# Eleven stage barriers of a four-layer graph network without GpSimd's drain

## The reference, cut to what matters

```python
edge_index = jnp.stack([src, dst])                       # 25,000 edges over 50,000 nodes
x = _layernorm(x + L0(x, W, gamma, beta, edge_weight, src, dst))      # weighted sum, matmul, norm, relu
x = _layernorm(x + L1(x, edge_index, edge_type_16, W1, root1, ...))   # two relational layers, mean per relation
x = _layernorm(x + L2(x, relation_emb, fc_w, fc_b, edge_index, edge_type_24, 2))  # two attention hops
x = _layernorm(x + L3(x, src, dst, edge_weight, W1, b1, W2, b2))      # interaction, leaky relu, unit length
```

## The kernel before, in words

| stage | what | Block | POOL's indirect DMAs |
|---|---|---|---|
| const | constants | L321 | none |
| sort | edges into buckets, records scattered | L475 | 380 scatters |
| weights | combined weights | L2272 | none |
| l0 | layer 0 | L815 | 410 gathers, 220 scatters between them |
| ma | messages of layer 1, first half | L992 | 216 gathers |
| l1a | relational layer | L1376 | 400 gathers |
| mb | messages, second half | L1255 | 216 gathers |
| l1b | relational layer | L1376 | 400 gathers |
| l2a, l2b | two attention hops | L1799 | 424 gathers each |
| l3 | layer 3 | L1536 | 402 gathers |

## Time and profile before

### The profile page before, as it was taken

How to read it: one execution, slowest core, us unless ns; L and a number is a source line. 1 busy time by engine, 2 the same in 40 slices (tenths; PEclk the granted TensorE clock), 3 DMA queues, 4 the chain that set the end, 5 groups by cost and what they waited for, 6 DMA issues and landing times. The chain is left out here.

```text
span 6966.6 us, 167248 instructions
## 1 busy us (share of the span) xinstructions
PE 6303.7 (90%) x37198; PEld 5105.5 (73%) x37199; DVE 5304.3 (76%) x18236; ACT 4305.0 (62%) x14812; POOL 3922.7 (56%) x3604
## 2 busy tenths in 40 slices
PE   5676899998789998989999899999899998999999
PEld 2222788887778887769999788888566666888887
DVE  9887889888646664247777677777688887899998
ACT  0000799996214443248888677777588887777777
POOL 6677777776736666754444444444444444444444
PEclk9555999999879999999999899999899999999999
DMA  1200677676656666667777566665577776444443
GB/s 40 6 2 3 200 197 198 194 197 200 186 158 193 197 198 186 196 189 222 222 222 222 172 189 188 187 187 173 169 222 218 216 215 187 119 128 127 127 127 118
DMA packets 1170067, 1165.56 MB, mean 167 GB/s; under 512 B 308723, under 2 KB 1044363, under 8 KB 1169182
## 3 DMA queue, kind: packets, MB, share of 16 engines
q1 hardware_dynamic: 1011934, 947.19, 44.3%
q0 software_dynamic: 158016, 217.06, 13.2%
HBM read 951.12 MB, written 396.74 MB: 193 GB/s over the span
## 5 line engine op out<-in xcount | busy, mean ns | idle before, releaser
L215 POOL DMA_INDIRECT l_gathered<-x,by_dst_meta x384 | 436.0, 1135 | 546.5 <-PE l_ps_a L1630 484.4
L1895 POOL DMA_INDIRECT l2b_gathered<-z,by_src_meta x408 | 430.5, 1055 | 532.2 <-PE l2b_ps_g L2138 416.6
L1895 POOL DMA_INDIRECT l2a_gathered<-x,by_src_meta x408 | 433.0, 1061 | 452.3 <-PE l2a_ps_g L2138 337.0
L215 POOL DMA_INDIRECT l1b_gathered<-messages,by_dst_meta x384 | 397.6, 1035 | 436.2 <-PE l1b_ps_b L1493 375.1
L215 POOL DMA_INDIRECT l1a_gathered<-messages,by_dst_meta x384 | 432.1, 1125 | 211.3 <-PE l1a_ps_b L1493 146.4
L712 PE MATMUL l2b_ps_x<-zero_row,ones_b 128*128 128x392 bf16 x2912 | 508.8, 329 | 0.0
L215 POOL DMA_INDIRECT l_gathered<-in_x,by_src_meta x384 | 414.0, 1078 | 119.6 <-issue 114.7
L924 ACT ACT_TABLE_LOAD x1 | 1.3, 1283 | 703.1 <-PEq L129 703.1
L1491 PE MATMUL l1b_ps_b<-root,l1b_x_t 128*128 128x256 f32 x1600 | 425.8, 389 | 0.0
L948 PE MATMUL l_ps_b<-l_w,l_both 128*128 128x256 f32 x1624 | 421.7, 383 | 0.0
L951 PE MATMUL l_ps_b<-l_w,l_agg_t 128*128 128x256 f32 x1624 | 420.0, 381 | 0.0
(11 more groups left out here) (402 smaller groups left out, 20752.6 us busy)
## 6 DMA issues: line engine op xcount, KB each, us to landing
l_both<-in_x_both SPq DMA_DIRECT2D x416, 256.0 KB
x<-l1b_result SPq DMA_DIRECT2D x400, 152.0 KB, 2.9
z<-l2a_result SPq DMA_DIRECT2D x400, 152.0 KB
l2a_x<-x SPq DMA_DIRECT2D x53, 1024.0 KB
l2b_x<-z SPq DMA_DIRECT2D x53, 1024.0 KB
x<-l_result SPq DMA_DIRECT2D x408, 128.0 KB
l1b_x<-h SPq DMA_DIRECT2D x408, 128.0 KB, 2.1
l1b_res<-x SPq DMA_DIRECT2D x408, 128.0 KB
```

The costliest lines, as they stand in the source:

```text
L215: pool.indirect_dma_start(gathered[:, slot, 0:D], None, source[0:count, :], bass.IndirectOffsetOnAxis(ap=rows, axis=0), bounds_check=limit ...
L1895: pool.indirect_dma_start(gathered[:, k, :], None, x_in[0:N_NODES, :], bass.IndirectOffsetOnAxis(ap=rows, axis=0), bounds_check=limit, oob ...
```

## The change

The first of the two meetings is asked for without GpSimd's drain, in all eleven Blocks. The same line changes in each place (L321, L475, L815, L992, L1255, L1376, L1536, L1799, L2272; the one at L1376 and the one at L1799 serve two stages each):

```diff
 def make_constants(nc, c):
     with Phase(nc, "const") as ph:
         made, numbered, spared = ph.sem("made"), ph.sem("numbered"), ph.sem("spared")
-        with nc.Block() as block:
+        with nc.Block(no_gpsimd_drain=True) as block:
             @block.vector
             def _(dve):
```

## The result

| | median us | lowest, highest | runs |
|---|---|---|---|
| before | 7686.9 | 7660.85, 7702.8 | 9 |
| changed | 7722.94 | 7699.82, 7745.0 | 9 |

The ratio is 1.005, with a 95% interval of 1.0035 to 1.0066: slower by 38 us (27 to 51), where 43 were forecast. In this document a cost in us with an interval is the ratio times the median of before; the medians themselves differ by 36.0 us here.

What follows compares the result with a forecast made beforehand. The bound inside stages was taken not to matter, only the joints between the eleven stages. Exposed second drains less first drains' path cost, 42.8 us, plus 0.3 for semaphores, took 7668.3 to 7711 us; range 7655 to 7730.

Steps and rivals of the forecast that it cites:

- The step that decided: Second meeting, behind the clears: POOL's long drain is fixed work starting with the drain, now paid uncovered; part of +43 us.
- Rival A: Second meeting: the drain only waits for an idle engine, so it takes 0.034 us; 7661 to 7662 us, chance 0.27.
- The terms: Second drains of nine stages, in order: 2.67, 3.49, 4.5, 6.27, 2.7, 6.27, 9.21, 9.21 and 6.43 us.
- The ninth, ma: Second drain of stage ma: 4.5 us, the tail of its first drain behind the last gather's end.
- The same reading of mb: Second drain of stage mb: 2.7 us, the tail of its first drain behind the last gather's end.
- Rival B: Second drains of ma and mb cost their recorded 7.2 and 18.3 us in full; 7729 us, chance 0.04.
- The part that comes off: First meetings: POOL drains on the path in sort, l1a and l2a (2.67, 1.96, 3.3) go, 7.9 us at most.
- The added semaphores: One more semaphore instruction on four engines at each of eleven meetings: 0.6 us at most, 0.3 taken.
- The sum: Whole program: second drains less what the first cost on the path, 42.8 us, plus 0.3 for semaphores: +43 us.
- the 701.7 us: Whole program: the median of the runs lies 701.7 us above the 6966.6 us span, for reasons outside the stages.

Runs made afterwards that it cites:

- the second trace of before: The kernel before, unchanged, traced once more: 6978.72 us with a span of 6977.0; two sets of runs beside it had medians of 6976.77 and 6975.95 us.
- the second trace of the same kernel: The changed kernel, unchanged, timed and traced once more: 7017.06 us against 6975.95 for the kernel before, ratio 1.006 (1.0047 to 1.0073).

## Why the prediction was right

**The step that decided was right.** It said that the long drain is work that starts with the drain, and so would be found by the second one. The rows of after settle it: in l1a the drain starts 9.4 us behind the end of the last gather (2860.9 - 2851.5), in l1b 23.9 us (4121.8 - 4097.9), and both take 6258 ns; in before these distances were 1.9 and 1.6 us, with 6268 ns. The runs with the place of the drain moved say the same of the time: put back ahead of the first meeting, it costs nothing. Rival A, for which the page of the Trainium skill spoke ("PSUM — Partial Sum Buffer", section "Engine vs sequencer instructions"), would have had 34 ns in all of them. In ma and mb the trace agrees with it: there the drain does wait for the queue. It doesn't give the 6258 ns of l1a and l1b, where all gathers had landed before the first meeting and the profile shows no POOL instruction that was left to wait for.

**The terms.** Nine second drains were forecast at 50.75 us and took 48.8; with the measured ones the sum would have been 48.8 - 7.9 + 0.3 = 41 us. Eight of the nine terms are right to 0.05 us. The ninth, ma, was mis-sized: 4.5 us forecast, 2.66 measured, because I took the whole tail behind the last gather, and up to 1.9 us of it was that gather's own landing, which is over by the second meeting. The same reading of mb came out at 2.7, and the drain took 2.65; but in the second trace of before the tails of ma and mb are 3.6 and 2.9 us, so a tail of this kind is no fixed price, and the close fit of mb is luck. Rival B, which took even more of these rows, would have been 18 us further off.

**The part that comes off,** the 7.9 us of first drains on the path, agrees with the kernel without any drain of POOL: 9.8 us (3.5 to 15), an interval too wide to check a stage. **The added semaphores,** 0.3 us, are below what can be measured: the kernel that has them, with the drain put back in its place, took 1.0003 of before.

**The sum,** +43 us, lies inside both measured intervals: 27 to 51 and 33 to 51. The absolute time, 7711, is 12 us under the 7722.9 measured, because it stands on the three runs with a median of 7668.3, where nine runs gave 7686.9. By the absolute time alone rival B (7729) would have come closer; it is the difference, and ma and mb on L129, that exclude it.

**What was wrong** is a step that did not carry the sum: that the 701.7 us between the span and the runs' median lie outside the stages. They lay inside them, and the recorded execution was 9% shorter than the runs. It did no harm because the large terms are durations that start and end with all engines standing, and none of those changed between 7013 and 7699 us. The 7.9 us are not of that kind, since they hang on when SP arrives; no trace of before at 7687 us shows them. For a term made of transfers or matmuls the harm would have hung on the stage: from one drain on L129 to the next, l2a takes 1330 us in the trace of after and 949 in the second trace of the same kernel, l2b 1174 and 1031, but l1b 907 and 898 and l3 1067 and 1066. So over half of the 686 us between the two spans lie in l2a, where the granted clock of TensorE was 0.78 against 0.98 and the DMA rate 127 against 179 GB/s. What makes the same program 10% longer (7687 against 6977 us) in one set of runs stays open; over the whole span the page of after has a mean DMA rate of 151 GB/s where that of before had 167, and a POOL about as busy (3866.0 against 3922.7 us).

## What to carry to other kernels

A GpSimd drain behind indirect DMAs is not only a wait but work, which starts with the drain: 2.7 to 9.2 us here, and some 82 ns for each gather since the last drain where these were under about 110. Two meetings in a row pay it once, in whichever comes first, so taking it out of the first only moves it to a place where all engines stand still. Either leave it where GpSimd arrives early, or take it out of both, if semaphores already order everything that one stage hands to the next; and where an instruction is cheap only because another of its kind stands ahead of it, price it as if that one were gone.

## What the runs showed of the hardware beyond that

The drain's length repeats to the nanosecond over traces while the program's time varies by 10%: the nine on L129 are the same in the two traces of the changed kernel, with spans of 7699 and 7013 us. Single gathers did not get slower in a program with no drain of POOL behind any of its 3492 indirect DMAs. And the 378 semaphore clears stand exposed between the two meetings in all of these kernels: the 32 of l1a run from 2858.8 to 2860.8 in the trace of after, 64 ns from one to the next. With 64 ns each, the 378 make an estimate of 24 us over the program. Fewer clears were not tried.
